# Causal mask of a six-layer local transformer: from an identity matmul on TensorE to a copy on ScalarE, with new engine orders

## What is computed

```python
q = l2norm(q) * qs
k = l2norm(k) * ksc
q = q * cos * scale + rotate_half(q) * sin * scale
k = k * cos * inv + rotate_half(k) * sin * inv
...
mask = (it < jb) | (it > jb + w) | (jb == -1)
sim = jnp.einsum('bhwie,bhwje->bhwij', bq, bk2) * QK_SCALE
sim = jnp.where(mask, -jnp.finfo(sim.dtype).max, sim)
attn = jax.nn.softmax(sim, -1)
out = jnp.einsum('bhwij,bhwje->bhwie', attn, bv2)
...
for i in range(DEPTH):
    x = attn_layer(shift_tokens(x), Wqkv[i], q_scale[i], k_scale[i], Wo[i]) + x
    x = ffn_layer(shift_tokens(x), ln_g[i], ln_b[i], W1[i], b1[i], W2[i], b2[i]) + x
```

## Time and profile before

| | |
|---|---|
| median of 3 runs | 4172.6 us (4172.09 to 4174.8) |
| profiled execution | 4169.85 us, of it a span of 4168.0 us |
| TensorE matmul busy | 3768.0 us, 90% |
| TensorE weight load busy | 3035.7 us, 73% |
| VectorE busy | 3089.8 us, 74% |
| ScalarE busy | 2730.3 us, 66% |
| GpSimd busy | 2299.0 us, 55% |

### The profile page before, as it was taken

The page is one execution under the profiler, slowest core; times in us unless marked ns, Lnnn a source line. Parts: engine busy times, 40 slices in busy tenths (PEclk is TensorE's granted clock), DMA queues, the critical chain, the costliest instruction groups (busy, mean ns, idle before and its releaser), DMA issues.

```text
span 4168.0 us, 144261 instructions
## 1 busy us (share of the span) xinstructions
PE 3768.0 (90%) x60560; PEld 3035.7 (73%) x60560; DVE 3089.8 (74%) x5783; ACT 2730.3 (66%) x5021; POOL 2299.0 (55%) x2139
## 2 busy tenths in 40 slices
PE   4747544799999999999999999999999999999998
PEld 3635533588887888878888778888788887877776
DVE  4385684777788777787777877778877778777773
ACT  2322122677777777777777777777777777776675
POOL 1000000766666666666666666666666666665662
PEclk9666565899999999999999999999999999999999
DMA  1000000333333433334333333333333333433332
GB/s 61 23 28 2 13 12 10 93 105 87 91 88 97 106 89 89 89 84 116 89 89 89 89 100 106 89 89 89 100 106 89 89 89 89 116 79 93 85 88 52
DMA packets 149484, 332.30 MB, mean 80 GB/s; under 512 B 17632, under 2 KB 27616, under 8 KB 147168
## 3 DMA queue, kind: packets, MB, share of 16 engines
q1 hardware_dynamic: 148832, 322.95, 29.3%
HBM read 218.02 MB, written 104.86 MB: 77 GB/s over the span
## 4 chain that ended last, share of the span: by engine, by line
PE 63%; ACT 13%; issue 4%; DVE 2%; POOL 1%; POOLq 0%; ACTq 0%; DVEq 0%
PE bank L1558 18%; PE bank L1645 9%; PE bank L1672 8%; PE bank L1614 7%; PE bank L1595 6%; PE bank L1660 4%; PE bank L1722 3%; PE bank L1629 3%; ACT L1221 3%; ACT L1223 2%; ACT gate L1221 2%; ACT pT L1155 1%; PE bank L1608 1%; ACT kT L1126 1%; PE bank L1697 1%
## 5 line engine op out<-in xcount | busy, mean ns | idle before, releaser
L1035 POOL TENSOR_TENSOR qk<-rot_a,rot_b 128x512 f32<-128x512 f32 x768 | 981.8, 1283 | 483.0 <-DVE rot_b L1365 474.7
L1045 POOL TENSOR_TENSOR qk<-qk,rn 128x512 f32<-128x512 f32 x768 | 785.6, 1050 | 109.0 <-DVE rn L1437 109.0
L1358 DVE TENSOR_TENSOR rot_a<-bank,rot 128x512 f32<-128x512 f32 x768 | 526.7, 686 | 299.3 <-PE bank L1558 287.9
L1115 ACT ACTIVATE sq<-bank 128x512 f32<-128x512 f32 x768 | 459.4, 598 | 268.3 <-DVE rot_b L1365 259.0
L1054 POOL TENSOR_TENSOR pr<-pr,prec 128x512 f32<-128x512 f32 x384 | 403.3, 1051 | 321.5 <-DVE prec L1402 321.5
L1558 PE MATMUL bank<-w_hi,xs_hi 128*128 128x512 f32 x1152 | 545.1, 473 | 35.9 <-POOL xs_lo L1025 18.3
L1373 DVE TENSOR_REDUCE ss<-sq 128x8 f32<-128x512 f32 x768 | 517.9, 674 | 36.8 <-ACT sq L1115 23.0
L1365 DVE TENSOR_TENSOR rot_b<-bank,rot 128x512 f32<-128x512 f32 x768 | 523.1, 681 | 0.0
L1595 PE MATMUL bank<-ident,qk 128*128 128x128 f32 x3072 | 467.9, 275 | 17.5 <-POOL qk L1045 10.9
L1558 PE MATMUL bank<-w_hi,xs_lo 128*128 128x512 f32 x1152 | 457.9, 397 | 0.0
L1558 PE MATMUL bank<-w_lo,xs_hi 128*128 128x512 f32 x1152 | 457.3, 397 | 0.0
(11 more groups left out here) (244 smaller groups left out, 7005.8 us busy)
## 6 DMA issues: line engine op xcount, KB each, us to landing
vw<-value_scratch SPq DMA_DIRECT2D x576, 256.0 KB, 4.9
value_scratch<-v SPq DMA_DIRECT2D x192, 512.0 KB, 2.8
vw<-value_scratch SPq DMA_DIRECT2D x192, 192.0 KB, 3.8
stage<-in_wqkv SPq DMA_DIRECT2D x6, 1536.0 KB, 9.5
stage<-in_wb_all SPq DMA_DIRECT2D x6, 1088.0 KB, 9.3
stage<-in_band SPq DMA_DIRECT2D x6, 512.0 KB, 5.0
d_xt<-in_x SPq DMA_DIRECT2D x4, 512.0 KB, 4.1
base_scratch<-d_res SPq DMA_DIRECT2D x4, 512.0 KB, 2.7
```

The lines of the kernel that those rows point to most:

```text
L1035: nc.gpsimd.tensor_tensor(qk[:, c, :], rot_a[:, c % 2, :], rot_b[:, c % 2, :], ALU.add)\
L1045: nc.gpsimd.tensor_tensor(y, y, rn[:, x.q, 8 * c:8 * c + 8].unsqueeze(2).to_broadcast([P, 8, DH]), ALU.mult).then_inc(S["scaled"], 1)
L1115: nc.scalar.activation(sq[:, :], proj_bank(x, c)[:, :], ACT.Square).then_inc(S["squared"], 1)
L1358: nc.vector.tensor_tensor(rot_a[:, c % 2, :].rearrange("p (h d) -> p h d", h=8), proj_bank(x, c)[:, :].rearrange("p (h d) -> p h d", h=8), ...
```

## The change

The identity matmul that writes the mask is kept for two units only (`unmarked`: units 0 and 1 of the first item). For all others a new ScalarE step `mask_scores(x, k)` copies the mask from SBUF into the bank, and `score` waits for it with the new semaphore `masked`. Besides, the steps of all four engines stand in a new order. `turn_output` now waits for one `turned_out` less, and the wait for `out_added` moves from chunk 6 to chunk 5.

```diff
+        def unmarked(x, k):
+
+            return x.u == 0 and k < 2
...
+            def mask_scores(x, k):
+
+                if not x.there or unmarked(x, k):
+                    return
+                need(act, S["shifted"], x.u * 4 + (k - 1))
+                nc.scalar.activation(ps_s[k % 2][:, :].rearrange("p (h n) -> p h n", h=NPAIR),
+                                     mask[:, k // 2, :].unsqueeze(1).to_broadcast([P, NPAIR, KEYS]), ACT.Copy)\
+                    .then_inc(S["masked"], 1)
...
-                if c == 6:
+                if c == 5:
                     need(pe, S["out_added"], x.u - (DEPTH - 1) * NSEQ - 2)
...
                 bank = ps_s[k % 2]
-                nc.tensor.matmul(bank[:, :].rearrange("p (h n) -> p h n", h=NPAIR), ident_b[:, :],
-                                 mask[:, half, :].unsqueeze(1).to_broadcast([P, NPAIR, KEYS]), start=True, stop=True)
+                if unmarked(x, k):
+                    nc.tensor.matmul(bank[:, :].rearrange("p (h n) -> p h n", h=NPAIR), ident_b[:, :],
+                                     mask[:, half, :].unsqueeze(1).to_broadcast([P, NPAIR, KEYS]), start=True, stop=True)
+                else:
+                    need(pe, S["masked"], x.u * 4 + (k + 1) - 2)
...
+                turn_output(b, ffn, turn.u * 8 + 5)
                 query_key(b, new, 6)
+                turn_qk(turn, 5)
+                turn_heads(att, 0)
                 score(att, 3)
                 turn_probs(att, 1, turn, 2)
+                turn_qk(turn, 6)
+                query_key(b, new, 7)
+                value(b, turn, 3)
+                score(turn, 0)
...
                 mean(out)
-                turn_qk(turn, 6)
-                query_key(b, new, 7)
-                value(b, turn, 3)
-                turn_qk(turn, 7)
-                turn_heads(att, 0)
                 weigh(att, 1)
+                turn_probs(att, 2, turn, 3)
                 variance(out)
-                turn_probs(att, 2, turn, 3)
-                score(turn, 0)
```

More of the change, by code:

```diff
@@ L1060, in body @@
                     low_half(new, "normed", out.u * 4 + 3)
+                elif att.there:
+                    low_half(new, "scaled", att.u * 8 + 8)
                 elif turn.there:
-                    low_half(new, "added", turn.u * 8 + 6)
+                    low_half(new, "added", turn.u * 8 + 7)
                 else:
                     low_half(new, "prepared", NPREP)
-                add(turn, 6)
                 add(turn, 7)
@@ L1257, in body @@
                         zero_values(i)
+                heads_out(out, 1)
+                heads_taken(out, 2)
                 exp(att, 0)
-                turned_out(turn, 0)
                 affine(ffn)
+                mask_scores(att, 2)
                 heads_out(out, 2)
-                value_out(turn, att, 0)
-                turned_out(turn, 1)
                 square(new, 1)
@@ L1267, in body @@
                         zero_values(i)
+                value_out(turn, att, 0)
                 gelu(ffn)
+                turned_out(turn, 0)
                 probs_out(out, 3)
@@ L1273, in body @@
                         zero_values(i)
+                turned_out(turn, 1)
+                heads_taken(out, 3)
+                mask_scores(att, 3)
                 turned_out(turn, 2)
-                turned_out(turn, 3)
                 value_out(turn, att, 1)
@@ L1280, in body @@
                         zero_values(i)
-                heads_taken(out, 3)
                 probs_out(att, 0)
-                turned_out(turn, 4)
-                heads_out(out, 3)
+                turned_out(turn, 3)
+                value_out(turn, att, 2)
+                if b.switch == -2:
+                    convert(b.layer, 4, "v_projected", turn.u * 4 + 3)
+                if b.switch == 1:
+                    need(act, S["y_done"], ffn.u + 1)
+                    nc.scalar.activation(w1[:, :, :, :].rearrange("p a c n -> p (a c n)"), stage_w1, ACT.Copy)\
+                        .then_inc(S["conv_act"], 1)
                 square(new, 4)
@@ L1290, in body @@
                     convert(b.next, 0, "projected", new.u * 8 + 5)
+                heads_out(out, 3)
                 exp(att, 1)
@@ L1298, in body @@
                     convert(b.next, 2, "projected", new.u * 8 + 6)
+                turned_out(turn, 4)
+                mask_scores(turn, 0)
                 exp(att, 2)
[L1300 to L1307, removed]
                 turned_out(turn, 5)
+                heads_out(att, 0)
                 square(new, 6)
@@ L1319, in body @@
                 turned_out(turn, 6)
-                square_centred(out)
+                shift_state(out)
                 value_out(turn, att, 3)
@@ L1545, in body @@
                 floors(new, out)
-                top(turn, 0)
+                shift(turn, 0)
                 if b.switch == -2:
@@ L1741, in body @@
                 query_key(b, new, 0)
+                turn_qk(att, 7)
+                score(att, 1)
+                turn_heads(out, 1)
                 weigh(out, 2)
-                turn_heads(out, 1)
-                score(att, 1)
                 spread(ffn)
-                turn_qk(turn, 0)
                 query_key(b, new, 1)
```

71 lines of the change are left out of this document (35 added, 36 removed).

## The result

The changed kernel takes 4125.66 us at the median (4123.62 to 4130.92, 4 runs), the kernel before 4173.09 us on the same chip (4172.09 to 4174.8, 4 runs). The ratio is 0.9888, interval 0.9871 to 0.9905: 47 us or 1.1% faster, where 1.8% was forecast. The profiled execution has a span of 4124.5 us, 43.5 less than before's.

The account below looks back on a forecast made before the run. It took TensorE's order, step behind step, as the bound. -88 - 22 + 59 - 25 = -76 us from the profiled 4169.85 gave 4094, and with the profile 2.75 under the median, 4097 us; range 4045 to 4160.

Parts of the forecast that it names:

- likeliest case: The forecast itself: 4097 us, own range 4080 to 4115, chance 0.50.
- the rival of small waits at more places: ScalarE's four more instructions per body and the body's edge cost another 0.2 to 0.7 us per body: 4116 to 4164; chance 0.22.
- The masks (-88 us): TensorE's stream: 382 mask matmuls go, at 0.23 us each, 0.92 us per body.
- The wait that goes (-22): TensorE's 0.23 us wait at `value(turn, 1)` for the copy into pT goes, in 96 bodies.
- The wait that comes (+59): TensorE waits 0.61 us per body at `turn_qk(turn, 1)` for `turned_out(turn, 0)`, now behind gelu's second table load.
- The edge: Body's end: GpSimd's add, scale, norm, `low_half` before the next body take 5.43 us against TensorE's 5.49; cost 0.
- One of the forecast's own signs of being wrong: At the next body's start: the forecast is wrong if `query_key(new, 0)` waits for `low_half` in every body.
- The last layer (-25): `turn_output` no longer idles 2.07 us for chunk 5's `turned_out` behind `shift_state`; -25 us, lower end -10.
- The wait was not absent: Rival: the new wait at `turn_qk(turn, 1)` does not come or is filled, only savings stay: 4038; chance 0.12.
- TensorE was the bound: Rival denied here: gaps between TensorE's weight loads are slack set by other engines, time stays at 4172.6; chance 0.06.
- The edge did bind: Rival: GpSimd's stretched steps at the body's end make `query_key(new, 0)` wait 1.6 us per body, +154, 4251; chance 0.10.

Follow-up runs that it names:

- the copy alone: Kernel before, old orders, with only the mask's copies moved to ScalarE at four places per body: 4149.89 us, ratio 0.9923.
- the kernel with both repairs: Changed kernel with the exp table load after gelu moved behind `heads_taken(att, 0)`, and `low_half` ahead of the scale of chunk 7: 4045.57 us, ratio 0.9675.
- the experiment that does it alone: Kernel before with only `turned_out(turn, 5)` moved ahead of `shift_state(out)` on ScalarE: 4145.5 us, ratio 0.9912.

## Why the prediction was right in direction and mechanism, and which terms were mis-sized

The gain, the mechanism and the place of the large wait came out as forecast, and the time lies in the range of 4045 to 4160. It lies outside the likeliest case's own 4080 to 4115 and inside the rival of small waits at more places (4116 to 4164). The sum was -76 us; the profiled spans show -43.5.

**The masks (-88 us): confirmed.** Without its waits the body before is 34.77 - 0.23 = 34.54 us, after 34.56 - 0.77 - 0.2 = 33.59: 0.95, or 0.24 us per mask, where 0.23 was taken; the copy alone gives 0.22, and so does the kernel with both repairs. The 131 ns of the Trainium skill ("TensorE: Matmul & The Clock Gate", section "Back-to-back issue gap") is not the price here; its 216 ns for an isolated matmul is near to it. And by the weight loads' share, one of the two measures for TensorE that the Trainium skill names ("Perfetto Trace Analysis", section "Identifying the Most-Contended Engine"), TensorE would have had 19% to spare; the trace does not agree, since what was taken out of the stream came back one to one, less the waits that took its place.

**The wait that goes (-22): confirmed** by TensorE's waits after, one for pT of 0.2 us in place of 93.

**The wait that comes (+59): right in place and releaser, too small.** It is 0.77 us, not 0.61, some +74. The chain of the other engines is 7.97 instead of 7.86, most of that in the last link: from the end of the copy (2511.28) to the transpose is 0.14 us, and I had read 0.05 off another place. TensorE's own way is 7.20 instead of 7.25. I had named the copy ahead of `heads_out` as the thing that could push the square back: at 2505.76 the queue and the rotations let the square go at the same time, so it costs nothing by itself, but nothing is left either, and one more copy there costs 0.42 us in each body.

**The edge ("No wait, but no slack either: cost 0"): the step that failed.** I had 5.43 us for GpSimd's chain against 5.49 for TensorE's. The timeline of GpSimd after, with the weight load that waits for it as the last row; the transposes of chunk 6 start at 2527.91, the projection at 2533.61:

```profile
2528.66 1.30 POOL L1039 TENSOR_TENSOR qk<-rot_a,rot_b 128x512 f32<-128x512 f32 x1 [1.20 <-PE bank L1614]
...
2529.91 1.05 POOL L1049 TENSOR_TENSOR qk<-qk,rn 128x512 f32<-128x512 f32 x1
...
2530.92 1.05 POOL L1058 TENSOR_TENSOR pr<-pr,prec 128x512 f32<-128x512 f32 x1
...
2532.11 0.73 POOL L1027 TENSOR_TENSOR xs_lo<-stateT,xs_hi 64x256 fp32r<-64x256 f32 x1
...
2532.91 0.64 POOL L1029 TENSOR_TENSOR xs_lo<-stateT,xs_hi 64x255 fp32r<-64x255 f32 x1
...
2533.60 0.19 PEld L1577 LDWEIGHTS bank<-w_hi,xs_hi 128*128 128x128 f32 x1 [0.18 <-POOL xs_lo L1029]
```

It is 5.70 us long: the add starts 0.75 after the transposes, not 0.65, and `low_half` 1.19 after the norm's start, not 1.01. Two starts of 0.1 and 0.18 us turned a slack of 0.06 into a wait of about 0.2, and taking it away gave 0.22 us per body and 0.55% of the time. The range had this as part of the rival of small waits; the point forecast had it at nothing. One of the forecast's own signs of being wrong, a wait of `query_key(new, 0)` for `low_half` in every body, thus came in most of them: the weight loads show it 72 times in some 88 bodies.

**The last layer (-25): confirmed**, -27 in the experiment that does it alone. After, `turn_output` costs a body 34.99 - 34.56 = 0.43 us, before 37.24 - 34.77 = 2.47.

**The sum again.** Per usual body -0.95 - 0.23 + 0.77 + 0.2 = -0.21 us, which is 34.77 to 34.56. The forecast had -0.54, and over 96 bodies the 0.33 between them are 32 us: 15 and 19 for the two mis-sized terms, less 3 for the masks' 0.95 in place of 0.92. 10 more lie ahead of the first `mean`. Against these 42 us stand 4 gained at the changes of layer (2.3 to 1.4 us, five times) and 3 in the two bodies of 38.77 us, none of which I had counted. That makes 35, where 32.5 is what the spans' difference of 43.5 lacks of the forecast 76. The remaining 2 or 3 us lie in the last three bodies, while the pipeline empties: they are 80.7 us before and 77.3 after.

**The rivals.** The wait was not absent. TensorE was the bound. The edge did bind, but by 0.2 us, not the 1.6 of stretched adds: they are 1286 ns in the mean. What came is the rival of small waits (0.22), in a mild form, 0.36 us per body of its 0.2 to 0.7: one more small wait, at the edge that it names, and the large one 0.16 us larger. That the two mis-sized terms alone so nearly give the miss is partly luck: two sums that I had not counted nearly cancel, 10 us ahead of the first `mean` and some 9 gained at the changes of layer, in the last layer and at the end. Neither would have put the time outside the range.

## What to carry to other kernels

When work is taken off the engine that bounds a hand-ordered pipeline, write down for each wait of that engine both ways to it, its own and the other engines'; what is freed on one of them is spent there up to their difference. A difference under some 0.3 us between two sums of ten links is no slack but a coin: give it a cost in the point forecast. And work moved to another engine is free by where it stands, not by that engine's busy share: here two copies off the chain cost nothing that shows and one on it 41 us, while moving a table load out of the chain was worth 77 us, 1.6 times the whole change.

## What the runs showed of the hardware

- ScalarE's copy of a bf16 mask from SBUF into a bank takes 596 ns at the median for 128x512, the same as its copies out of a bank (0.60), and the next instruction starts 0.52 us after it.
- A pause of 2.1 us of TensorE, one in a body of 37 us and with the engine at work before and behind it, was followed by a stretch at the 1.2 GHz level in some bodies and by none in others; so was a wait of 1.4 us, at three of five changes of layer. In windows of 100 us between 3600 and 4000 us the clock is 0.93 to 0.98 in parts of the last layer of the kernels with the pause, and 1.00 throughout in those without. Such a pause can cost twice its own length (about 2 us of idleness, and up to 2.5 more in 39.5 against 37.0).
- Copies and squares run at the same 0.60 us with gelu's table set loaded as with exp's, so the load back can wait until the next exp.
